# One core, 48 attention and feed-forward units: the planner's table of durations is rewritten from the trace, stage by stage

## What is computed

```python
x = x + attn_a(layernorm(x), ...)   # 8 heads of 64, low-rank keys and values, full softmax over 512 tokens
x = x + ffn(layernorm(x), ...)      # two inner layers: local attention (window 128, rotary), then a gated feed-forward
x = x + attn_b(layernorm(x), ...)   # 16 heads of 16, causal, scores = dot^2 / (|q|^2 + |k|^2 - 2 dot + eps)
x = x + ffn(layernorm(x), ...)      # the same two inner layers again
```

## Time and profile before

| | |
|---|---|
| median of 3 runs | 5082.77 us (5076.04 to 5086.52) |
| profiled execution | 5068.32 us, span 5066.3 us |
| PE busy | 4401.1 us, 87% of the span |
| DVE busy | 3392.7 us, 67% |
| ACT busy | 2583.0 us, 51% |
| POOL busy | 2323.3 us, 46% |
| granted PE clock, mean | 0.924 of full speed |

### The profile page before, as it was taken

The page is one execution under the profiler, slowest core; times in us unless marked ns, Lnnn a source line. Parts: engine busy times, 40 slices in busy tenths (PEclk is TensorE's granted clock), DMA queues, the critical chain, the costliest instruction groups (busy, mean ns, idle before and its releaser), DMA issues.

```text
span 5066.3 us, 65767 instructions
## 1 busy us (share of the span) xinstructions
PE 4401.1 (87%) x23008; PEld 2677.9 (53%) x23008; DVE 3392.7 (67%) x7648; ACT 2583.0 (51%) x5513; POOL 2323.3 (46%) x2203
## 2 busy tenths in 40 slices
PE   7888888999999999987787777777799999999997
PEld 3444445555555555554554454444555555555564
DVE  4454466666666666647889988999766666656553
ACT  4344344444444444427887777777444444444442
POOL 1111145455454454534555555565545444455441
PEclk9999999999999999997777777887899999999998
DMA  2000000000001000000000000100000000000000
GB/s 65 9 5 5 9 22 11 3 3 5 20 3 31 7 9 11 16 16 17 20 20 17 16 22 18 32 11 15 29 3 3 5 20 9 25 15 17 11 15 21
DMA packets 61208, 77.56 MB, mean 15 GB/s; under 512 B 13896, under 2 KB 45264, under 8 KB 60880
## 3 DMA queue, kind: packets, MB, share of 16 engines
q1 hardware_dynamic: 60880, 73.36, 5.0%
HBM read 35.61 MB, written 12.58 MB: 10 GB/s over the span
## 4 chain that ended last, share of the span: by engine, by line
PE 61%; DVE 21%; issue 7%; ACT 6%; POOL 4%; DMA 1%; SPq 1%; DVEq 0%; POOLq 0%; ACTq 0%
PE wide L725 44%; PE o_ps L725 8%; PE turn_ps L728 5%; PE wide L728 3%; DVE prob L1262 3%; DVE x L1256 2%; DVE pt L1299 2%; DVE prob L1273 2%; DVE hid L1256 1%; DVE x L1143 1%; DMA shifted<-resid 1%; DVE st L1280 1%; ACT pt L1106 1%; POOL rn L1443 1%; DVE w_up L1239 1%
## 5 line engine op out<-in xcount | busy, mean ns | idle before, releaser
L1477 POOL TENSOR_SCALAR prob<-prob,st 128x256 f32<-128x256 f32 (+1 forms) x1024 | 524.8, 533 | 976.9 <-DVE st L1286 976.6
L725 PE MATMUL wide<-x,w_up 128*128 128x512 f32 (+5 forms) x2560 | 943.5, 593 | 21.6 <-DVE k_t L1203 11.4
L725 PE MATMUL wide<-w_in,x_t 128*128 128x512 f32 (+1 forms) x1792 | 828.9, 607 | 6.5 <-DVE w_up L1246 3.1
L725 PE MATMUL o_ps<-pt,v 128*64 128x256 f32 (+2 forms) x5632 | 619.7, 369 | 118.6 <-DVE pt L1299 77.0
L1106 ACT ACTIVATE pt<-turn_ps 128x512 f32<-128x512 f32 x384 | 229.2, 597 | 854.1 <-PE turn_ps L728 854.1
L725 PEld LDWEIGHTS o_ps<-pt,v 128*64 128x64 f32 (+1 forms) x5632 | 394.6, 140 | 380.1 <-issue 191.2
L1075 ACT ACTIVATE prob<-prob,st 128x256 f32<-128x256 f32 (+1 forms) x1024 | 479.0, 472 | 194.7 <-DVE st L1273 194.5
L728 PE MATMUL turn_ps<-ident,prob 128*128 128x128 f32 x2816 | 465.3, 285 | 125.6 <-ACT pt L1106 121.9
L725 PEld LDWEIGHTS wide<-x,w_up 128*128 128x128 f32 (+2 forms) x2560 | 365.1, 200 | 375.5 <-issue 354.4
L728 PEld LDWEIGHTS turn_ps<-ident,prob 128*128 128x128 f32 x2816 | 315.1, 142 | 420.1 <-issue 238.0
L725 PEld LDWEIGHTS wide<-w_in,x_t 128*128 128x128 f32 x1792 | 339.9, 200 | 370.4 <-issue 363.8
(11 more groups left out here) (132 smaller groups left out, 7823.2 us busy)
## 6 DMA issues: line engine op xcount, KB each, us to landing
kept<-resid SPq DMA_DIRECT2D x16, 512.0 KB, 2.6
x<-kept SPq DMA_DIRECT2D x16, 512.0 KB, 3.3
w_up<-hid SPq DMA_DIRECT2D x64, 128.0 KB, 2.2
x<-hid SPq DMA_DIRECT2D x64, 128.0 KB, 2.3
shifted<-resid SPq DMA_DIRECT2D x32, 224.0 KB
w_in<-in_f_wqkv SPq DMA_DIRECT2D x4, 1536.0 KB, 6.4
w_up<-in_f_w SPq DMA_DIRECT2D x4, 1364.0 KB, 6.3
resid<-in_x SPq DMA_DIRECT2D x8, 512.0 KB, 8.1
```

The lines of the kernel that those rows point to most:

```text
L725: return eng.matmul(out, lhsT, rhs, start=start, stop=stop, skip_group_check=True)
L1477: last = eng.tensor_scalar(pr[:, local_span(t)], pr[:, local_span(t)], sm[:, 8 + t:9 + t], 1.0, ALU.mult, ALU.mult)
```

## The change

The numbers in `B_COST` and `cost()` are replaced; no instruction is added or removed and no dependence is changed. For `b` the duration of `bmul` goes from 0.8 + 0.6 to 0.8 + 0.88 us for each 128 columns (2.6 to 3.44 us at 384 columns); for `f` the duration of `score` and of `mix` from 2.8 us to 1.72 and 1.68 us. Most others move by a tenth or two.

```diff
-B_COST = {"bclip": (0.15, 0.27), "bnum": (0.1, 0.22), "bguess": (0.2, 0.47), "bclose": (0.2, 0.6), "bmul": (0.8, 0.6),
+B_COST = {"bclip": (0.3, 0.27), "bnum": (0.1, 0.23), "bguess": (0.2, 0.48), "bclose": (0.2, 0.58), "bmul": (0.8, 0.88),
...
     if kind in ("score", "mix") and st != "b":
-        return 2.8 if i % 2 else 0.0
+        return {"score": {"a": 1.92, "f": 1.72}, "mix": {"a": 2.4, "f": 1.68}}[kind][st] if i % 2 else 0.0
```

More of the change, by code:

```diff
@@ L94 @@
         ENGINE[_k] = _e
-B_COST = {"bclip": (0.15, 0.27), "bnum": (0.1, 0.22), "bguess": (0.2, 0.47), "bclose": (0.2, 0.6), "bmul": (0.8, 0.6),
-          "exp": (0.85, 0.21), "turn_a": (0.03, 0.175), "turn_b": (0.03, 0.175), "pt_a": (0.06, 0.12),
-          "pt_b": (0.12, 0.135), "mix": (0.05, 0.34), "mask": (0.95, 0.0)}
+B_COST = {"bclip": (0.3, 0.27), "bnum": (0.1, 0.23), "bguess": (0.2, 0.48), "bclose": (0.2, 0.58), "bmul": (0.8, 0.88),
+          "exp": (0.85, 0.24), "turn_a": (0.03, 0.17), "turn_b": (0.03, 0.17), "pt_a": (0.1, 0.12),
+          "pt_b": (0.13, 0.135), "mix": (0.05, 0.33), "mask": (1.14, 0.0)}
 def cost(kind, u, i):
@@ L109, in cost @@
     if kind in ("bden", "bdot"):
-        return 0.05 + 0.38 * b_width(i) / P if kind == "bdot" else 0.0
+        return 0.05 + 0.34 * b_width(i) / P if kind == "bdot" else 0.0
     by_stage = {
-        "low": {"a": 1.3, "f": 2.2}, "exp": {"a": 1.6, "f": 2.9}, "inv": {"a": 0.9, "f": 0.15}, "wt": {"a": 1.2, "f": 2.2},
-        "turn_a": {"a": 0.6, "f": 0.6}, "turn_b": {"a": 0.6, "f": 0.45}, "pt_a": {"a": 0.65, "f": 0.65},
-        "pt_b": {"a": 0.65, "f": 0.6}}
[3 rows of a table added]
     if kind in by_stage:
         return by_stage[kind][st]
[L117 to L125, removed]
+    flat = {"xt": 0.95, "qk": 3.7, "vv": 3.7, "spread": 0.93, "aq": 3.7, "lat": 1.85, "ak": 1.9, "av": 1.9, "bqkv": 3.7,
+            "bk": 0.65, "bq": 0.65, "proj": 1.72, "xt2": 1.06, "up_g": 3.55, "up_h": 3.55, "down": 2.6, "sel": 0.65,
+            "xt_c": 1.2, "raw": 2.04, "v_c": 1.03, "q_c": 0.6, "aq_c": 1.03, "lat_c": 0.6, "av_c": 1.03, "bsq": 0.93,
+            "bk_c": 0.57, "bq_c": 0.57, "out": 0.6, "olog": 1.2, "out_b": 2.4,
+            "gelu": 5.6, "bn_h": 2.3, "nrm_h": 1.5, "cos": 2.08, "ss": 1.62, "join": 2.63, "k_c": 0.68, "ak_c": 1.23,
+            "row": 0.95, "bss": 0.8, "res": 1.23,
+            "bn_f": 1.11, "bn_f2": 1.79, "nrm_f": 2.9, "xt2_c": 1.6, "gate": 1.49, "hid": 1.49, "res2": 1.23,
+            "rstd_h": 1.02, "sin": 3.14, "rn": 3.05, "brow": 1.8, "bias_b": 2.4,
+            "rstd_f": 1.01, "bias": 2.38, "back": 2.5, "rot": 4.0, "pad_out": 1.0, "pad_down": 0.3, "pad_v": 4.0}
     return flat.get(kind, 0.2)
```

## The result

| | before | changed |
|---|---|---|
| median of 10 runs | 5075.95 us (5068.01 to 5089.0) | 5101.09 us (5093.08 to 5113.88) |
| profiled execution | 5068.32 us | 5095.11 us, span 5093.1 us |
| ratio | | 1.0048, 95% interval 1.0033 to 1.0063 |

The changed kernel is slower by 25 us, 0.5%. The page of the changed kernel, against the earlier trace rows: DVE is busy 149 us more, and no other engine is: PE 32 us less, ACT and POOL within 12.

A forecast was written before the change was run, and what follows sets the result against it. PE was taken to set the pace in f, DVE in b. Gains of 45 us in f and 49 us in b, -94 us from 5082.8, gave 4989 us; 4905 to 5070 us was to hold 8 in 10.

The forecast's parts named there:

- the first wait: Stage f, PE: turn_b7 waits 2.1 us a unit for pt_a7; order unchanged, so it stays.
- the new one at `turn_b0`: Stage f, PE: turn_b0 would wait 0.7 us a unit for the single turn_ps buffer.
- The sum is -1.1 - 0.6 - 0.6 - 0.4 + 0.7 = -2.0 us: Stage f: net PE waits per unit in 16 units, -1.4 us in the other 16, together -54 us.
- rival 4: More than the sum: b gives 75 us, f 64 us, a higher clock 27 us; kernel at 4917 us; 15%.
- Rival 3: Stage f gives nothing, its waits return at spread1 for rn0 or at turn_a4; kernel at 5034 us; 13%.
- my -45: Stage f: total gain forecast, the -54 us less a sixth for seams and parts that become late next.
- My lower bound: Stage f: no gain at all, since each removed wait comes back as another.
- `join0` ahead of `cos1` at no cost: Stage f, DVE: cos1 starts some 1.5 us later, ss1 about 1 us earlier; costed at nothing.
- I take three quarters of the 57.5 us as gone: Stage b: DVE's waits for PE (bdot 40.7, turn 16.8 us in seven units) mostly go, giving -49 us.
- rival 1: Stage b: port lock stretches bmul beside POOL's bclose, costing 48 us; f at half its gain; kernel at 5109 us; 10%.
- rival 2: Stage b: port lock costs 0.25 us more a step, b gives nothing, f its 45; kernel at 5038 us; 17%.
- 0, give or take 15 us: Stage a, the seams between stages and the transfers: no net change expected.

The follow-up runs named there:

- `pair_f_only`: Kernel before, with new durations for a and f only, and score halves taking buffers only when both can: 5021.18 us, ratio 0.9891.
- `pair_old`: Kernel before, old durations everywhere, with the planner rule that score halves take buffers only when both can: 5070.28 us, ratio 0.9984.
- `pair_new`: Changed kernel, with the planner rule that outside b score halves take buffers only when both can: 5049.39 us, ratio 0.9944 of the kernel before.
- `f_only`: Kernel before with the new durations for stages a and f, the old ones for b: 5081.61 us, ratio 1.0009.
- `bmul_back`: Changed kernel with bmul alone back at its old duration of 0.6: 5103.64 us, ratio 1.005 of the kernel before.
- `nolock_after`: Changed kernel with bclose's multiply on POOL replaced by two memsets that only write: 4911.83 us, ratio 0.9673 of the kernel before.
- `wr_after`: Changed kernel with each bclose multiply on POOL replaced by three memsets, about as long together: 4934.54 us, ratio 0.9727 of the kernel before.
- the best version: Kernel before, with new durations for a and f only, and score halves taking buffers only when both can: 5021.18 us, again 5019.73 us.

## Why the prediction was wrong

I forecast 4989 us, 94 us faster; it is 25 us slower, 0.5%.

**f, the waits that go.** Right one by one: those for `nrm_f`, for `pt_b` at `mix1`, for `res` and for `k_t` are gone, the first wait stays at 2.08 us, and the new one at `turn_b0` is 0.74 us where I said 0.7.

**f, the sum.** The step that failed is "The sum is -1.1 - 0.6 - 0.6 - 0.4 + 0.7 = -2.0 us": its only new wait was that of `turn_b0`. For each moved part I asked whether the work in front of it covers its inputs, not which buffer it would write and who still reads that. Two waits for buffers, 1.79 + 1.18 = 3.0 us, took the place of the 2.7 us removed. By these terms a unit should be 1.0 us longer; it isn't, since the PE work of nearly every unit is now 86.3 us, at clock 1.00, where many had 88.1.

I had read from those rows that half of the units are at 0.98, which rival 4 uses; it is 6 of 12 in the first two `f` stages, but 10 of 11 in the last two. Rival 3 had the result (f gives nothing) but other places (`spread1`, `turn_a4`).

With the buffer freed, the new durations of `a` and `f` bring 49 us (`pair_f_only` against `pair_old`), close to my -45, but the likeness is luck: its PE waits are others (16.5 us for `k_t` in 9 waits up to 2.0), and in the traces, one of each, only 18 of the 41 us between the two lie from the `res` of 9 to 23 and 33 to 47; 11 lie between 23 and 33. My lower bound, "each wait comes back as another", was what happened; I gave it 13%. Of the two buffer waits the one of `vv1` comes from the early `score4`, as `pair_new` shows; the one at `up_h1` comes from what no longer stands between `up_h0` and `up_h1`, which is read from the lists and not tested.

**f, DVE.** `join0` ahead of `cos1` at no cost: nothing in PE's waits contradicts it. DVE is busier, though (L1180 means 1147 ns for 997, L1143's 128x128 rows 612 and 579 for 342 and 341), by work that now lies elsewhere beside POOL: of those 128x128 rows in the whole changed trace, the ones with POOL idle take 0.35 us at most, and those beside `sin` (L1435) up to 1.45.

**b, the waits that go.** "I take three quarters of the 57.5 us as gone": 33.6 us are left (19.7 + 13.9), so 42% went. The wait for `pt_b`, of which I wrote "so this wait goes", went from 54.2 to 39.2 us only, and those for `bclip` grew, from 37.5 to 101.0 us (L1241) and from 10.3 to 43.9 (L1246). The waits for POOL stayed, as assumed (22.3 to 21.3).

**b, DVE's own time.** The step that failed was to count waits that go as time won, with `bmul` at its old length. From the `res` of unit 24 to that of 30 the reductions take 333 us before and 385 after, 0.36 us a step; in the first unit 59 and 95 us. That is more than the waits gave. I named this as rivals 1 and 2, and as the sign by which to know them a rise of the means of L1262 and L1256 by more than a fifth: the mean of L1262's reductions rose by 22% (853 to 1040 ns over all; in the groups shown 42% at 384 columns, 30% at 256, 10% at 512), and L1256's did not rise (1141 to 1022 at 768 columns). I had written against rival 1 that "most of POOL's 736 us in this stretch must fall beside it as it is". It did, but from 230 to 326 us beside the reductions was still room. The loss per step is under the 0.5 us from which rival 1 was to decide; with `f` at nothing, it was enough for the sign. `b`'s middle came out as rival 2 has it (b gives nothing) and `f` as rival 3; I had priced them one at a time and not both together, and what makes it slower are the two ends of `b`.

**The rule on the port.** With the reads of `bclose` taken away, the reduction of 512 columns takes 741 ns for 1252 and the new order of `b` loses 2 to 8 us for 23 to 28 (traces; by the medians 5, 11 and -1 for 25, 25 and 28). So the engines don't meet at semaphores alone, as the first section has it. The Trainium skill (SBUF — State Buffer, "Who interferes with whom") says that a DVE instruction with two SBUF inputs contends with a GpSimd instruction that reads SBUF, and not with one that only writes it. By that rule the memsets would not stretch it; the trace agrees, as the 138 reductions with only memsets beside them show, 0.68 to 0.70 us, under a POOL that is busier than before (693 us of 1120 for 655).

**The seams.** I gave them "0, give or take 15 us", and named "if the seams between `f` and `b` lose tens of us" as what would prove me wrong: they lose 11.5 and 9.6 us. The entry is the reads. The exit isn't, it is there with memsets alone (+16 to +17); its cause stays open. Whether the two stages' changes cost more together (25) than apart (4 + 7) is open too.

## What to carry to other kernels

- When a planner's table is made truer, look at what its wrong numbers were hiding. Here a part of length zero took a buffer: with its partner 10 us behind, mending it gave 6 to 8 us; with 24 us, 52. For every moved part ask which buffer it gets, and who reads that last.
- Where the bound is an engine's own busy time, a list of its waits is no budget. Ask what its instructions will lie beside; the new order removed 24 us of DVE's waits and added 28 us of busy time in 1120 us (1013 to 1041).
- The larger prize was beside the question: POOL's reads in `bclose`, with what follows from them, cost 150 us, six times what the order did.
- A duration that is changed for one unit moves the parts of the units behind it. Before a kernel is read as "only this unit changed", compare the lists; and a few us in one stretch of one trace say little where unchanged lists differ by 7.

## What was not expected of the hardware

- A POOL that only writes leaves DVE's two-input reductions alone: 128x512 at 0.68 to 0.70 us, as with an idle POOL; beside POOL's multiplies they take up to 2.3, and one of 384 columns 2.70 us. A normalisation of 128x128 (L1143), which reads one tile and two numbers a row, stretches beside a multiply too, from 0.34 to 1.45 us. A multiply on POOL over 768 columns takes 2.03 us, a memset of it 0.74.
- PE's granted clock was 1.00 in all but two of the changed trace's 23 full `f` units, with waits of 2.08, 1.79, 1.18 and 0.74 us in each; it is so, but for one or two units, in the traces of the four other kernels with these `f` lists too (`f_only`, `bmul_back`, `nolock_after`, `wr_after`). Before, with waits of 2.1, 1.1 and less, 16 of 23 units were at 0.98, and the best version's `f` stretches are at 0.98 too, with PE busier (1245.04 of 1315 us). More idle time went with the higher clock; I have no explanation that a run here tests.
